# Folding a bias into the last product on TensorE, and ReLU with the residual add into one VectorE operation

## What is computed

```python
h = relu(bn(concat([x[src], edge_attr]) @ W1 + b1))        # 53125 x 128
agg = mean of h over the edges that end in a node           # 3125 x 128
h2 = relu(bn(concat([x, agg]) @ W2 + b2))                   # 3125 x 256
y = relu(h2 @ Wl + bl)                                      # 3125 x 128
out = layernorm(x + y, axis=-1)
```

## Time and profile before

| what | value |
|---|---|
| time, median of 3 runs | 711.31 us (710.66 to 714.36) |
| the profiled execution's own time | 711.14 us |
| its span, first to last instruction | 709.3 us |
| busy: PE / VectorE / ScalarE / GpSimd | 63% / 55% / 27% / 65% of the span |
| mean granted TensorE clock | 0.628 of full |

### The profile page before, as it was taken

One profiled execution on the slowest core, in us unless ns is written; L12 is line 12 of the kernel. 1 busy time (PEld: TensorE's weight loads), 2 busy tenths in 40 slices (PEclk: granted clock), 3 DMA queues, 4 the chain that ended last, 5 costly groups with the idle time before them and its releaser, 6 DMA issues.

```text
span 709.3 us, 11010 instructions
## 1 busy us (share of the span) xinstructions
PE 448.4 (63%) x2195; PEld 342.3 (48%) x2195; DVE 389.3 (55%) x801; ACT 191.0 (27%) x517; POOL 458.1 (65%) x572
## 2 busy tenths in 40 slices
PE   6665556565655556566655565656554389999943
PEld 5543334443443334344433344434442389999643
DVE  4445454545454544554554545454544667777796
ACT  1111212212121212121211122121212245666445
POOL 2377777777777777777777777777777223333643
PEclk9855555555555555555555555555555599999978
DMA  6333334434333334344333344343333365878103
GB/s 179 103 111 93 111 103 118 118 111 118 112 104 105 108 106 118 111 118 118 110 93 111 104 118 118 111 118 111 105 103 84 99 205 148 238 224 228 44 0 91
DMA packets 64845, 83.91 MB, mean 118 GB/s; under 512 B 19539, under 2 KB 43524, under 8 KB 64829
## 3 DMA queue, kind: packets, MB, share of 16 engines
q1 hardware_dynamic: 39885, 39.07, 19.1%
q0 software_dynamic: 13312, 27.29, 15.8%
q10 hardware_dynamic: 11632, 17.39, 6.8%
HBM read 63.61 MB, written 20.08 MB: 118 GB/s over the span
## 4 chain that ended last, share of the span: by engine, by line
POOL 41%; DMA 18%; PE 16%; issue 15%; DVE 7%; ACT 1%; DVEq 0%; ACTq 0%; SPq 0%; POOLq 0%
POOL res L600 30%; POOL work L600 11%; DMA work<-ytab,srci 9%; DMA spill<-work 7%; PE psH L764 7%; PE psC L764 6%; DVE work L1041 2%; PE psH L696 2%; DMA hotb<-hot_dram 1%; DVE res L1173 1%; PE psT L821 1%; DMA res<-in_x 1%; DVE res L1242 1%; PE psC L680 0%; DVE res L1175 0%
## 5 line engine op out<-in xcount | busy, mean ns | idle before, releaser
L600 POOL DMA_INDIRECT res<-ytab,srci x312 | 297.1, 952 | 116.6 <-issue 94.8
L716 PE MATMUL psH<-w1e,work 128*128 128x256 f32 x416 | 212.7, 666 | 157.5 <-ACT work L847 157.5
L716 PEld LDWEIGHTS psH<-w1e,work 128*128 128x128 f32 x416 | 121.1, 321 | 216.5 <-ACT work L847 197.9
L861 ACT ACTIVATE work<-res 128x512 f32 (+1 forms) x78 | 49.1, 629 | 333.1 <-DVE res L1041 201.7
L1041 DVE TENSOR_TENSOR res<-psH,res 128x512 f32 (+1 forms) x78 | 53.9, 691 | 144.5 <-DMA res<-ytab,srci 137.0
L600 POOL DMA_INDIRECT work<-ytab,srci x104 | 98.9, 951 | 31.7 <-issue 31.7
L1055 DVE TENSOR_TENSOR psX<-work,psX 128x512 f32<-128x512 f32 x104 | 72.2, 694 | 28.3 <-ACT work L861 28.3
L1142 DVE TENSOR_TENSOR work<-res,psX 128x512 f32<-128x512 f32 x103 | 70.7, 688 | 26.4 <-PE psC L764 13.3
L618 POOL TENSOR_TENSOR agg<-agg,srci 128x64 f32 x104 | 32.0, 308 | 66.4 <-ACT srci L908 66.0
L710 PE MATMUL psT<-ident,work 128*128 128x128 f32 x208 | 64.0, 410 | 1.9 <-DVE col L1013 1.9
L728 PE MATMUL psC<-hotb,onesb 128*128 128x64 bf16 x416 | 26.5, 239 | 58.0 <-DVE hotb L1020 58.0
(11 more groups left out here) (146 smaller groups left out, 380.4 us busy)
## 6 DMA issues: line engine op xcount, KB each, us to landing
work<-in_edge_attr SPq DMA_DIRECT2D x103, 128.0 KB, 2.1
hot_dram<-hotb ACTq DMA_DIRECT2D x26, 256.0 KB, 2.0
spill<-work ACTq DMA_DIRECT2D x26, 256.0 KB, 2.2
res<-spill SPq DMA_DIRECT2D x25, 256.0 KB, 3.1
res<-ytab,srci POOLq DMA_INDIRECT x312, 2.5
hotb<-hot_dram SPq DMA_DIRECT2D x13, 256.0 KB, 2.7
work<-hot_dram SPq DMA_DIRECT2D x13, 256.0 KB, 2.9
h2x_dram<-agg ACTq DMA_DIRECT2D x25, 125.0 KB, 2.4
```

Source lines behind the costliest of these rows:

```text
L600: pool.indirect_dma_start(rows[:, j * F:(j + 1) * F], None, ytab, bass.IndirectOffsetOnAxis(ap=srci[:, j, g:g + 1], axis=0)).then_inc(gath ...
L716: last = pe.matmul(psH[q % 2][:, b * 2 * F:(b + 1) * 2 * F], eat[:, q % 2, b * P:(b + 1) * P], w1e[:, :, :].rearrange("p a f -> p (a f)"), ...
L861: act.activation(sq[:, q % 2, :], slot(i, q), ACT.Square).then_inc(sq_ready, 1)
```

## The change

TensorE adds `bl` itself: for each tile it multiplies an identity of 125 x 125 with the tile `blr` (bl in all of its 125 rows) into the bank, and the two products with Wl are accumulated on it. The four banks of the first batches get this `bias` ahead of the loop, once all 14 adds of L1173 are over; from batch 4 on it is issued just before the batch's own products. VectorE then makes `max(psum, 0) + x` in one operation (`out_relu`, in place of `out_max`) for every batch. GpSimd's multiplication (L643), its 25 additions (L646) and its five (L653) are gone, and so are VectorE's two (L1233), the tile `nbl` and three semaphores. PE now waits on the semaphore of the new operation before it writes a bank again. The number of products on PE rises by 25, which is 50 records.

```diff
@@ gpsimd
-            pool.wait_ge(s_nodein, NODEIN)
-            pool.tensor_scalar(nbl[0:PN, :], blr[0:PN, :], -1.0, None, ALU.mult).then_inc(s_bl, 1)
-            for t in range(NT):
-                rows = xn[0:PN, t * F:(t + 1) * F]
-                last = pool.tensor_tensor(rows, rows, blr[0:PN, :], ALU.add)
-            last.then_inc(s_bl, 1)
-            pool.wait_ge(s_bl, 2)
-            for b in POOL_Z:
-                t0, n = BATCH[b]
-                zb = z[0:PN, t0 * F:(t0 + n) * F]
-                pool.wait_ge(s_relu, b + 1)
-                pool.tensor_tensor(zb, zb, xn[0:PN, t0 * F:(t0 + n) * F], ALU.add).then_inc(s_z, 1)
@@ tensor
+            def bias(b):
+
+                for t in range(BATCH[b][1]):
+                    pe.matmul(BANK[b % 4][0:PN, t * F:(t + 1) * F], ident[0:PN, 0:PN], blr[0:PN, :], start=(t == 0),
+                              stop=False)
+
             pe.wait_ge(s_h2, len(prods))
+            pe.wait_ge(s_nodein, NODEIN)
+            for b in range(4):
+                bias(b)
             for b, (t0, n) in enumerate(BATCH):
                 pe.wait_ge(s_h2r, b + 1 if b < DVE_RELU else H2 * (b + 1) - DVE_RELU)
                 pe.wait_ge(s_h2rd, min(b + 1, DVE_RELU))
                 if b >= 4:
-                    pe.wait_ge(s_relu, b - 3)
+                    pe.wait_ge(s_z, b - 3)
+                    bias(b)
                 for t in range(n):
                     o = BANK[b % 4][0:PN, t * F:(t + 1) * F]
                     for h in range(H2):
                         n0 = h * N + (t0 + t) * PN
-                        last = pe.matmul(o, h2r[:, n0:n0 + PN], wl[:, h * F:(h + 1) * F], start=(h == 0),
-                                         stop=(h == H2 - 1))
+                        last = pe.matmul(o, h2r[:, n0:n0 + PN], wl[:, h * F:(h + 1) * F], start=False,
+                                         stop=(t == n - 1 and h == H2 - 1))
                 last.then_inc(s_ops, 1)
@@ vector
-            def out_max(b):
+            def out_relu(b):
 
                 t0, n = BATCH[b]
                 dve.wait_ge(s_ops, b + 1)
-                dve.tensor_tensor(zv[:, t0:t0 + n, :],
-                                  BANK[b % 4][0:PN, 0:n * F].rearrange("p (t f) -> p t f", t=n),
-                                  nbl[0:PN, :].unsqueeze(1).broadcast_to([PN, n, F]), ALU.max).then_inc(s_relu, 1)
-                if b not in POOL_Z:
-                    zb = z[0:PN, t0 * F:(t0 + n) * F]
-                    dve.wait_ge(s_relu, b + 1)
-                    dve.tensor_tensor(zb, zb, xn[0:PN, t0 * F:(t0 + n) * F], ALU.add).then_inc(s_zd, 1)
+                dve.scalar_tensor_tensor(out=z[0:PN, t0 * F:(t0 + n) * F], in0=BANK[b % 4][0:PN, 0:n * F], scalar=0.0,
+                                         in1=xn[0:PN, t0 * F:(t0 + n) * F], op0=ALU.max, op1=ALU.add).then_inc(s_z, 1)
 
             def row_stats(b):
                 t0, n = BATCH[b]
-                if b in POOL_Z:
-                    dve.wait_ge(s_z, POOL_Z.index(b) + 1)
-                else:
-                    dve.wait_ge(s_zd, b + 1 - sum(k < b for k in POOL_Z))
+                dve.wait_ge(s_z, b + 1)
@@
-            dve.wait_ge(s_bl, 2)
```

More of the change, by code:

```diff
@@ L69, in gnn_kernel @@
     DVE_NORM = [int(3 <= b < len(BATCH) - 1) for b in range(len(BATCH))]
-    POOL_Z = list(range(1, len(BATCH) - 1))
     XLOADS = [BATCH[0:1], BATCH[1:2], BATCH[2:4], BATCH[4:]]
@@ L165, in gnn_kernel @@
         blr = head(F)
-        nbl = head(F)
         zo = head(NT * F)
@@ L275, in gnn_kernel @@
         s_ops = sem("out_psum")
-        s_relu = sem("out_relu")
         s_z = sem("z_ready")
-        s_zd = sem("z_ready_dve")
         s_sqrt3 = sem("ln_sqrt")
         s_ln = sem("ln_scale_ready")
-        s_bl = sem("bl_in_x")
         s_rst = sem("row_stats")
@@ L1272, in norm_last @@
                                       ALU.add).then_inc(s_zod, 1)
-            dve.wait_ge(s_bl, 2)
             NBT = len(BATCH)
             for b in range(NBT + 2):
-                steps = [(out_max, b), (rstd, b - 2), (row_stats, b - 1), (shift, b - 2), (join_stats, b - 1),
+                steps = [(out_relu, b), (rstd, b - 2), (row_stats, b - 1), (shift, b - 2), (join_stats, b - 1),
                          (norm_last, b - 2)]
                 if b == 1:
-                    steps = [(row_stats, 0), (join_stats, 0), (out_max, 1)]
+                    steps = [(row_stats, 0), (join_stats, 0), (out_relu, 1)]
                 for step, batch in steps:
```

## The result

The changed kernel takes 702.86 us (median of 6 runs, 702.48 to 705.09), the kernel before 711.84 us in the same comparison: ratio 0.9871, 95% interval 0.9848 to 0.9894. It is faster by 9.0 us; the two profiled executions differ by 8.5 us of span, and the rest lies in the scatter between runs. The direction was right, the size was not, and the profile shows which part of the size.

The account below looks back on a forecast made before the run. It took VectorE's chain in the last 40 us as the bound. Gains of 2.59, 0.53, 0.72, 1.1, 0.88 and 0.24 us, less 1.2 for new waits on PE, made 4.9: 706.4 us, range 704.9 to 709.2.

Parts of the forecast that it names:

- What bounds the kernel now: Whole span: only about the last 40 of 709.3 us can move, with VectorE the chain there nearly all the way.
- The sum: Up to `rstd(4)`: all gains less new waits on PE give 4.9 us, so 706.4 us.
- Part 1: Ahead of the loop: without GpSimd's 26 operations L1182 falls from 2.76 to 0.17 us, gaining 2.59.
- Part 2: Ahead of the loop: 32 bias records on PE take 3.54 us, covered by the statistics chain, at full clock.
- Part 3: PE in the loop: batches 0 to 3 take 1.77 us each, later ones 2.65; VectorE's new waits cost 1.2.
- Part 4: VectorE in the loop: `out_relu` takes L1227's 0.65 to 0.69 us, `shift` 0.15; `rstd(4)` moves 4.9 us earlier.
- The clock rival: PE's clock falls in the pauses around the bias ahead of the loop: gain 3.2 us, time 708.1, chance 0.14.
- L1182 was held by GpSimd: Rival ahead of the loop: L1182 wasn't held, its 2.59 us stays; gain 2.3, time 709.0, chance 0.06.
- `out_relu` doesn't cost its two parts: Rival in the loop: `out_relu` costs both its parts, 1.38 us; gain 1.7, time 709.6, chance 0.08.
- PE kept 2.4 GHz through the loop: Rival in the loop: PE stays at 1.2 GHz and bounds it; 6.8 us slower, 718, chance 0.04.

Follow-up runs that it names:

- dead_additions: Changed kernel with GpSimd's multiplication and 25 additions put back, into a tile nothing reads: 870.0 us, kernel before beside it 872.6; repeated, 712.8 against 716.2.
- dead_products: Kernel before with 25 identity products on PE, results unused, ahead of the last product: 869.7 us, kernel before beside it 872.6.
- no_bias: Changed kernel without the bias products, so bl is left out of the last layer: 867.4 us, kernel before beside it 872.6.
- before_again: Kernel before, unchanged, run once more: 869.8 us, kernel before beside it 870.8.
- one_addition: Kernel before with GpSimd's 25 additions of bl as one operation: 868.3 us, kernel before beside it 870.8.
- scale_only: Changed kernel with GpSimd's wait for the node inputs and its multiplication of bl by -1, result unused: 704.5 us, kernel before beside it 716.2.
- subtraction: Kernel before with GpSimd making -bl by a write of zeros and a subtraction, not the multiplication: 875.2 us, kernel before beside it 875.2; ratio 1.0002.

## Why the prediction was wrong

**What bounds the kernel now**: this is the step that failed. "Nothing edited runs before the last window sum, so of the 709.3 us of the span only about the last 40 can move." The first half is true, the second doesn't follow from it: 3.5 us moved before that point. Removing the multiplication of L643 made the 416 gather issues shorter, 3.1 us in all, and they are on the chain. The sum had put the edge part at nothing, only because no edited line lies in it. With 3.1 us more it would have been 703.3, outside its range and close to the 702.86 measured. Why the multiplication does this stays open.

**Part 1** was right: 0.17 us for L1182, 2.59 us gained, and dead_additions brings the wait back to 2.77 us, ending with the last addition. One remark of the prediction has little behind it: it says that L1227 keeps its 0.65 to 0.69 us "beside both" kinds of GpSimd's additions. L646 was over before the first L1227, and only the one at 692.47 overlaps an addition of L653, by 0.17 us. No term of the sum rests on it.

**Part 2** was right: 32 records in 3.58 us (3.54 forecast), covered by the statistics, pauses of 1.76 and 0.81 us, clock at 2.4 GHz. dead_products and no_bias show its two sides: the bias pays for itself by keeping the clock, by 0.5 us at `rstd(4)`.

**Part 3** was right: the waits moved to batches 4 and 5 with 0.44 and 0.68 us, 1.1 against 1.2.

**Part 4** was right: `out_relu` 0.68 us, `shift` 0.15. `rstd(4)` starts at 693.05, 32.70 us into the node part, where it was 37.66: 5.0 us earlier, 4.9 forecast.

**The rivals.** None of the four came true. The clock rival is real all the same: it was hit twice in three runs once the pause had grown from 0.8 to over 3.2 us. L1182 was held by GpSimd, `out_relu` doesn't cost its two parts, and PE kept 2.4 GHz through the loop.

## What to carry to other kernels

Ask what GpSimd's elementwise work does to VectorE where both run at once: here a back-to-back stream of it held a VectorE TENSOR_SCALAR of two elements until it ended, though not the TENSOR_REDUCE just ahead, and no wait in the code shows it. Look for rows whose duration doesn't fit their size. Products that fill a pause ahead of a burst on PE can cost nothing and give the clock back. And when a time moves by more than the edited part, split the span at the first edited operation before explaining anything: here the two halves had different causes, and one of them shows in time only on some chips.

## What the runs showed that I had not expected

- One GpSimd multiplication by a constant near the end of the program makes every indirect DMA issue ahead of it longer: shortest into `res` 947 to 948 ns in the 7 traces with it (before, before_again, one_addition, dead_products, both dead_additions, scale_only), 938 to 943 in the 13 without. Why stays open: the gathers' own instructions are the same, and the program has another operation of this kind, with two factors, in all of the kernels. I didn't try the multiplication on other data or in another place.
- 25 additions of 128 elements take 10.4 us on GpSimd, one of 3200 elements 7.0.
- After a pause of PE of 3.2 to 3.4 us, 2.4 GHz was kept in one trace and lost in two, one of them of the same program.
- On some chips the same kernel takes some 160 us longer. In the trace of subtraction, on such a chip, ScalarE stands still 24 times in the edge part, 12.5 us on average, for something that the profile doesn't name.
